# Token layers of a two-part network with fewer unread products on TensorE

## The reference

```python
h = layernorm(x, ln1_g[i], ln1_b[i])
q = softmax(split(h @ Wq[i]) * DH ** -0.25, axis=-1)   # over the features of a head
k = softmax(split(h @ Wk[i]) * DH ** -0.25, axis=-2)   # over the tokens
v = split(h @ Wv[i])
context = einsum('bhnd,bhne->bhde', k, v)
x = x + einsum('bhnd,bhde->bhne', q, context) @ Wo[i] + bo[i]
h = layernorm(x, ln2_g[i], ln2_b[i])
x = x + gelu(h @ W1[i] + b1[i]) @ W2[i] + b2[i]
```

## Time and profile before

| what | us |
|---|---|
| three runs without the profiler | 785.52, 787.54, 792.06 |
| median | 787.54 |
| the profiled execution, its own time | 793.09 |
| its span, from the first to the last instruction | 791.3 |
| TensorE matmul busy | 645.8 (82%) |
| VectorE busy | 555.0 (70%) |
| ScalarE busy | 359.9 (45%) |
| mean granted clock of TensorE | 0.931 |

### The profile page before, as it was taken

How to read it: one execution, slowest core, us unless ns; L and a number is a source line. 1 busy time by engine, 2 the same in 40 slices (tenths; PEclk the granted TensorE clock), 3 DMA queues, 4 the chain that set the end, 5 groups by cost and what they waited for, 6 DMA issues and landing times. The chain is left out here.

```text
span 791.3 us, 22405 instructions
## 1 busy us (share of the span) xinstructions
PE 645.8 (82%) x10251; PEld 431.9 (55%) x10251; DVE 555.0 (70%) x802; ACT 359.9 (45%) x485; POOL 49.9 (6%) x88
## 2 busy tenths in 40 slices
PE   3799954767999747669899289998968989898997
PEld 2777731335776513338666133345447878787754
DVE  7768878994589869964798778936218675757462
ACT  0025559500155578000456488635014747474763
POOL 4000000002000000020000000020001111110200
PEclk9999987999699959995999699999989999999999
DMA  8101000013010000040110000130050000000001
GB/s 321 22 22 63 2 1 1 2 41 122 14 52 22 2 0 2 1 161 3 42 42 2 0 2 2 41 122 22 15 193 1 2 1 1 1 2 1 1 1 29
DMA packets 12271, 27.29 MB, mean 34 GB/s; under 512 B 3472, under 2 KB 4368, under 8 KB 12176
## 3 DMA queue, kind: packets, MB, share of 16 engines
q1 hardware_dynamic: 11888, 25.12, 9.4%
q10 hardware_dynamic: 288, 0.73, 0.3%
HBM read 24.80 MB, written 1.05 MB: 33 GB/s over the span
## 5 line engine op out<-in xcount | busy, mean ns | idle before, releaser
L450 ACT ACTIVATE V<-ps,wts 128x1024 f32<-128x1024 f32 x96 | 101.8, 1111 | 242.6 <-PE ps L803 242.6
L624 DVE BATCH_NORM_STATS2 stats<-V 128x6 f32<-128x512 f32 x192 | 117.9, 676 | 16.5 <-ACT V L450 16.5
L500 DVE STREAM_TRANSPOSE A<-V 128x2048 f32<-128x2048 f32 x48 | 107.3, 2275 | 6.7 <-ACT V L399 6.7
L399 ACT ACTIVATE V<-V,small 128x2048 f32<-128x2048 f32 x48 | 96.7, 2083 | 5.0 <-DVE small L652 5.0
L696 PE MATMUL ps<-A,tab 128*128 128x384 f32 x192 | 73.1, 519 | 30.9 <-DVE A L507 30.9
L684 PE MATMUL ps<-A,tab 32*32 32x512 f32 x1536 | 67.2, 646 | 25.4 <-DVE A L500 25.4
L696 PEld LDWEIGHTS ps<-A,tab 128*128 128x128 f32 x192 | 34.9, 195 | 79.1 <-DVE A L507 57.2
L803 PEld LDWEIGHTS ps<-tab,A 64*128 64x128 f32 x1024 | 59.6, 188 | 29.6 <-issue 25.2
L507 DVE STREAM_TRANSPOSE A<-ps 128x1024 f32<-128x1024 f32 x48 | 56.7, 1222 | 20.5 <-PE ps L684 20.5
L618 DVE STREAM_TRANSPOSE A<-ps 128x2048 f32<-128x2048 f32 x24 | 55.6, 2317 | 20.3 <-PE ps L746 20.3
L803 PE MATMUL ps<-tab,A 64*128 64x128 f32 x1024 | 65.8, 278 | 2.0 <-DVE A L618 2.0
(11 more groups left out here) (233 smaller groups left out, 903.3 us busy)
## 6 DMA issues: line engine op xcount, KB each, us to landing
A<-in_modes SPq DMA_DIRECT2D x32, 384.0 KB, 4.3
r_ky<-in_modes SPq DMA_DIRECT2D x16, 384.0 KB, 3.0
wl<-in_layers SPq DMA_DIRECT2D x3, 452.0 KB, 5.8
wm<-in_mixture SPq DMA_DIRECT2D x1, 874.5 KB, 8.1
tab<-in_table SPq DMA_DIRECT2D x1, 656.5 KB, 4.7
A<-in_turned SPq DMA_DIRECT2D x1, 512.0 KB, 3.6
V<-in_pixels SPq DMA_DIRECT2D x4, 128.0 KB
tower_out<-A SPq DMA_DIRECT2D x2, 256.0 KB, 2.9
```

The costliest lines, as they stand in the source:

```text
L399: nc.scalar.activation(pair, pair, ACT.Relu, bias=bias, scale=scale).then_inc(s_relu, 1)
L450: nc.scalar.activation(Vm[:, 2 * h:2 * h + 2, r, 512 * q:512 * (q + 1)], bank(half_of_u(q, r) + 2 * h, 2).rearrange("p (m n) -> p m n", m= ...
L500: nc.vector.transpose(T[n % 3].rearrange("p (k n) -> p k n", k=16), Vk[:, :, P * n:P * (n + 1)]).then_inc(s_T, 1)
L624: last = nc.vector.bn_stats(stats[:, 16 * q + 4 * r + m, :], Vm[:, m, r, 512 * q:512 * (q + 1)])
```

## The change

It takes out two of the four places at which `warm` is called: the two products ahead of the first variances of the second, third and fourth layers, and the four behind the turn of q of group 1 in each of the four layers. The three and two products at the turns of k stay. That is 22 of 42 products, 44 of 84 instructions.

```diff
@@ -1521,8 +1521,6 @@
 
             for l in range(DEPTH):
                 w = wl[:, l, :]
-                if l:
-                    warm(2)
                 variance(l, 0)
                 pe.wait_ge(s_wl[l], 16)
                 for g in range(G):
@@ -1548,8 +1546,6 @@
                     for t in range(GP):
                         last = nc.tensor.transpose(bank(g, 0, GW + P * t, P), part(qs, g)[:, P * t:P * (t + 1)], ident)
                     last.then_inc(s_qtr, 1)
-                    if g == 1:
-                        warm(4)
                 for g in range(G):
                     pe.wait_ge(s_kqT, l * G + g + 1)
                     pe.wait_ge(s_vs, l * G + g + 1)
```

## The result

| | us |
|---|---|
| before, four runs | 785.52, 787.54, 792.06, 795.87; median 789.8 |
| after, three runs and the profiled one | 799.55, 800.09, 800.36 and 815.34; median 800.23 |
| ratio after to before | 1.0108, 95% interval 1.0055 to 1.0161 |
| span of the profiled execution after | 813.5 |

By the ratio the change makes the kernel 1.1% slower, 8.5 us of 789.8 (the two medians lie 10.4 us apart); the forecast was 797.0 us, +9.5 us on 787.54. The profiled execution after, which the ratio leaves out, is some 15 us longer than the other three, since in the tower, which the change does not touch, its clock stood at half for 37 us, and the token part begins 14 us later. So I compare the token part alone: from TensorE's first instruction in it (585.42 before, 599.49 after) to the end of the span. It grows from 205.9 to 214.0 us, by 8.1 us.

What follows compares the result with a forecast made beforehand. TensorE was taken to set the pace, except in the softmax, waiting for VectorE. 3 x 1.1 + 1 x 6.0 + 1 x 1.7 - 1.4 = +9.6 us on the 787.54 median: forecast 797.0 us, range 785.8 to 808.5.

Steps and rivals of the forecast that it cites:

- The central step: Gap behind the turn of q: without its products the clock falls in each of four layers, 0 to 6.9 us each.
- the second term: Gap ahead of the first variances: one clock fall in the three layers, costing 1.7 us.
- The gains: Products no longer delaying work: 0.9 us ahead of the first variances, 0.5 us behind the turn of q, together 1.4 us.
- The 0.5 us in the second layer: Second layer's turn of q: without the late four products, 0.5 us gained of a 0.7 us delay.
- The short fall: Behind the turn of q: half clock for some 3.4 us costs 1.1 us, in three of four falls.
- The long fall: Behind the turn of q: half clock through contexts and outputs costs 6.0 us, in one of four falls.
- the 32-column products of the earlier trace: In the tower before: clock at half for 17 us though TensorE was busy; taken as evidence for long falls.
- the clock holds: Rival, token layers: no more falls than now, only the gains left, 786.1 us; chance 0.15.
- long falls in most layers: Rival, behind the turn of q: clock at half until the 256-column products of L1575 or L1582, +21.3, 809 us; chance 0.10.
- Short falls only: Rival, behind the turn of q: four layers fall, contexts bring the clock back, +3.0, 790.5 us; chance 0.27.

Runs made afterwards that it cites:

- the second trace: The changed kernel measured again with the same code, against the kernel before: 1.0135; token part 215.4 us.
- the first trace: The first profile of the changed kernel, both places taken out, against the kernel before: 1.0108; token part 214.0 us.
- the second edit alone: Only the four products behind the turn of q taken out of the kernel before: 1.0143, and 1.0039 when measured again.
- the first 1.005 and 1.0004: Only the two products ahead of the first variances taken out of the kernel before: 1.005, and 1.0004 when measured again.
- the k gap filled: The changed kernel with five instead of three unread products behind the turn of k of group 1: 1.0143 of the kernel before.

## Why the prediction was right, and where it was not

**The central step held.** The four products behind the turn of q lay in idle time and cost nothing, and without them the clock is at half at the contexts in three and in four of four layers, where I took four. It gets there in two ways, and I had reckoned with one of them: in the second trace the gap itself brings the clock down, in the contexts; in the first, the clock falls behind the turns of k, as it can before the change, and stays down. In the first layer of the first trace the gap of 2.18 us did nothing. The signs that I had named came in part: a layer was to take 39.5 us, or 44, and took 40.06 to 41.26; L1510 was at half clock behind more than one of the first variances, which was to mean that the second term was too small.

**The gains.** Predicted 0.3 us per layer ahead of the variances; a layer without a fall takes 38.17 us instead of 38.50, so 0.33. The 0.5 us in the second layer cannot be seen by itself: that layer fell again.

**The short fall.** Predicted 1.1 us, measured 1.2 (39.71 - 38.50).

**The long fall failed.** The term "1 x 6.0" supposed that half clock lasts through the contexts and L1566. In no trace did it. The long stretches, of 6.8 to 10.2 us, began earlier, behind the turns of k, and covered the waits for VectorE: the turn of q at half clock takes 1.12 us instead of 0.66, but its end moves by only 0.5 us. They ended at the latest 1.4 us into the outputs. A layer with 10.2 us at half clock loses 2.45 us (40.95 - 38.50 with the second edit alone, 40.63 - 38.17 in the trace after: 0.46 at the last turn of q, 1.73 in the contexts, 0.26 in the outputs). One with 6.8 us loses only about 1.0 us (40.74 - 38.17, less 1.6 for the fall behind the variances in the same layer). The contexts, with 128 columns an instruction, are followed by the way back in every case; the 32-column products of the earlier trace rows were the wrong row to go by (and from 206.5 us on that stretch held products of 128 and of 512 columns too, on a part of the array).

**Ahead of the variances the price was right and the count was not.** Predicted one fall in three layers at 1.7 us. L1510 took 3.60 us instead of 1.97, so 1.6; but there were two and three falls, 1.6 to 3.2 us more than I had. In the sum this error and the one before nearly cancel, and that was luck: the forecast came close with one term at least 3.5 us too large and another too small. By the second trace: 4 x 1.2 + 3 x 1.6 - 3 x 0.33 = 8.6 us, and 0.6 less as the fall of before is gone from its place: 8 us of the 9.5 between the two token parts (215.4 - 205.9). That trace has two more stretches at half clock behind the fourth layer's turns, from 754.6 and from 761.4 on, at places that the change leaves alone. In the first trace after only 6.1 of the 8.1 us lie between the first turn of k and the last normalization's variances; 0.5 us come ahead of the first turn of k, where the clock was at half for longer than before, and 1.2 us in the last normalization.

**Of the rivals**, *the clock holds* and *long falls in most layers* are out. *Short falls only* had the right mechanism behind the turn of q in the second trace; its sum of +3.0 lacked the falls behind the variances.

**The parts do not add.** With the products at q in place, taking out the others brought a fall behind the variances in 2 of 6 layers; with those gone too, in 8 of 9. I had counted the two places separately. The times alone would not show it: the second edit gave 1.0143 and 1.0039, the first 1.005 and 1.0004, both 1.0108 and 1.0135. In the second trace after, and with the k gap filled, the falls repeat every 40.96 us at the same place of each layer, a layer being just as long as that: a layer that has lost time at both places puts the next one's gaps where they fall again. That this is how one edit makes the other dearer fits all traces but was argued from them, not tried by itself.

## What to carry to other kernels

Here unread products in a wait cost nothing as long as they ended before the wait did, and what they bought did not show in their own place but in the products behind it. Judge them by the granted clock over the next few microseconds, and fit their number to the idle time on both sides: too many delay the chain (0.33 us here), too few leave the fall to chance. Where a kernel repeats the same layer, look at two traces at least, since the same gap brings the clock down in one and not in another.

## What the runs showed of the hardware

- The gap of 2.18 us at the turn of q, entered at full clock, brought the clock down in 12 of 15 layers (0 of 1 and 4 of 4 in the two traces after, 2 of 2 and 2 of 4 with the second edit alone, 4 of 4 with the k gap filled). So the same instructions at the same times within a layer do not decide it. With the four products in it the gap was entered at full clock in 17 layers of five traces and brought it down in none, with two products in none of three.
- Behind the first variances the clock fell in 10 of 15 cases with no unread product ahead, in none of 6 with one and in none of 18 with two.
- Sixteen instructions of two columns, 1.85 us busy, did not hold the clock in two of the three layers whose gap was entered at full clock; seven turns of 128 columns, 0.93 us with 1.42 us of idle time behind them, held it in two of two and let it come back in a third, where 1.11 and 1.70 us of turns were nearly all of TensorE's work.
- At half clock the contexts take 3.0 to 3.8 us instead of 2.06, and the outputs, which VectorE paces at full clock (4.16 us), take 3.79 us behind a slow stretch.
- In the tower the clock stood at half for 37 us in one execution while TensorE was busy for all of it (37.00 of 37.00 us).
